# Three rounds of graph message passing on one core: a new order of the first blocks, larger first transfers and products of a constant at the beginning

## The chip, the cores and the metric

The kernel runs on one core of a Trainium2 chip. Its time is the device time of one execution in microseconds, as the median of several runs. An execution with the hardware profiler gives the trace; it has a span of its own, from the first to the last recorded event. Engines are called TensorE (PE in the rows, PEld for its weight loads), VectorE (DVE), ScalarE (ACT), GpSimd (POOL) and SyncE (SP, which here only issues DMAs).

## What is computed

x is 4096 x 128, adj is 4096 x 4096, both f32. A layer on a graph, a residual and a layer norm come first, then three rounds of two MLPs of three layers (without the last "vu" MLP, whose result is not used), a residual and a layer norm:

```python
x = _layernorm(x + relu((adj @ x) @ kernel + bias))
u = x
for _ in range(3):
    v = _mlp(adj @ u, uv_W1, uv_b1, uv_W2, uv_b2, uv_W3, uv_b3)
    u = _mlp(adj @ v, vu_W1, vu_b1, vu_W2, vu_b2, vu_W3, vu_b3)
return _layernorm(x + v)
```

Each multiplication with adj needs all of its 64 MB. There are six of them one after the other.

## The kernel before

**Blocks and uses.** adj is cut into 8 x 8 blocks of 512 x 512 (1 MB, 128 partitions of 2048 values). A *sweep* s is one multiplication with adj; row r of it makes chunk r of the result, and block (r, c) multiplies chunk c of the features. adj doesn't fit on the core, so a block that is loaded is used for sweep s ("finish") and, where the features of sweep s + 1 are there already, for that sweep too ("begin"). `block_products` lists these *uses*; for sweep 0 they stand in the table FIRST, written out by hand. There are 384 uses in all. Use n takes the ticks 4n to 4n + 3, a tick for each of the block's four tiles; all engines run over the same ticks in their own program.

**A use.** [...] A half of a block (two tiles, 128 x 1024) is copied by ScalarE from `adj_raw` to `adj_hi` (L593), and VectorE writes the difference to `adj_lo` (L722). TensorE multiplies adj_hi with feat_hi (L858) and feat_lo (L865) for two tiles, and then adj_lo with feat_hi (L872) for both: six products of 512 columns for a half, twelve for a use. The first block that needs a chunk of x brings it along (`brings_x`): x goes to `resid`, and is split by ScalarE (L587) and VectorE (L718).

**Buffers and queue.** `adj_raw` holds RAW = 8 halves, `adj_hi` and `adj_lo` hold RING = 4 blocks. SyncE issues all loads in the order of `plan.loads`. It waits until VectorE is through with the half that stood in the slot before; for the first WHOLE = 8 blocks one transfer brings both halves, and waits for both.

**Where the copies stand.** `Plan.due` gives the tick at which ScalarE and VectorE take up a half: its first use less a lead of FIRST_LEAD = 4 ticks for uses under 24 (FIRST_ROWS rows of 8), of LEAD = 12 ticks after that, and not before its place in the ring is free. Within a tick the steps of units come ahead of the halves in both programs. Whatever comes first in a program holds up what is behind it.

**Units.** When a row is closed, its chunk goes as a *unit* through the layers. For sweep 0 (kind GCN) the steps, counted in ticks from the tick after the close, are: ScalarE copies the bank (0), TensorE multiplies with the kernel (3, L769: four products of 128 columns), VectorE adds the bias (3, L689), adds the residual and takes mean and variance (5, L652, L606, L610), ScalarE takes the root (7, L518), VectorE scales (9, L617, L621), ScalarE writes feat_hi (11, L501) and VectorE feat_lo (12, L635). In the order before, units 0, 1, 2 and 3 close at uses 14, 16, 26 and 36 (counted from 0). Uses 19, 20, 24, 29, 30 and 37 are the ones that take a block already there.

Of the kernel before, what the change touches and what calls it, by code (L numbers as in the profile page):

```python
# [9 lines left out]
P = 128  # L10
# [16 lines left out]
DEEP = HIDDEN + (LAST,)  # L27
FINISH, BEGIN = "finish", "begin"

FIRST = (("finish", 1, (0,)), ("finish", 0, (6, 5, 1, 0)), ("finish", 2, (7,)), ("finish", 0, (7, 4, 3)),  # L30
         ("finish", 1, (7, 5, 2, 6, 1)), ("finish", 0, (2,)), ("finish", 1, (4, 3)), ("finish", 2, (0, 6)),
         ("begin", 2, (0,)), ("begin", 1, (0,)), ("finish", 2, (1, 4, 3)), ("begin", 2, (1,)),
         ("finish", 2, (5, 2)), ("finish", 3, (0,)), ("both", 3, (1,)), ("begin", 3, (0,)),
         ("finish", 3, (7, 4, 3, 6, 5)), ("both", 3, (2,)), ("finish", 4, (0, 1)), ("begin", 4, (0,)),
         ("finish", 4, (2, 7, 6, 5, 4, 3)), ("begin", 4, (1, 3, 2)), ("both", 5, (0, 1, 2, 3)),
         ("finish", 5, (7, 6, 5)), ("both", 5, (4,)), ("both", 6, (0, 1, 2, 3, 4)), ("finish", 6, (7, 6)),
         ("both", 6, (5,)))
WHOLE = 8
HOLD = 3
LEAD, FIRST_LEAD, FIRST_ROWS = 12, 4, 3  # L40
LOAD_GCN, LOAD_PARAMS = 24, 90
W_SPLIT = 320

# [27 lines left out]
def block_products(rows):  # L71
# [20 lines left out]
    for s in range(PASSES - 1):  # L92
        if s == 0:
            for what, r, columns in FIRST:
                yield from dict(finish=finish, begin=begin, both=both)[what](s, r, columns)
# [25 lines left out]
class Plan:  # L121


    def __init__(self, rows):
# [61 lines left out]
        for h, (b, i, _) in enumerate(self.loads):  # L186
            if b >= WHOLE or i == 0:
                signals[h % RAW] += 1
# [4 lines left out]
        for h, (b, i, pieces) in enumerate(self.loads):  # L193
            for j in range(pieces):
                self.load_at[b, i + j] = h
            first = self.first_use(b)
            free = 0 if self.before[b] is None else self.ends[self.before[b]] * TILES + i + pieces
            lead = FIRST_LEAD if first < FIRST_ROWS * rows else LEAD
            due = max(free, first * TILES + i - lead)
            turns = [t for (step, t), u in self.steps.items() if step == "dve_in" and self.steps_of(u) == TURN]  # L200
            self.due.append(next((t for t in turns if t - HOLD < due < t), due))
# [69 lines left out]
def gnn_kernel(nc, x, adj, weights, bias_rows, out):  # L271
# [12 lines left out]
    with ctx:  # L284
        def sb(name, shape, dt=F32):
            return ctx.enter_context(nc.sbuf_tensor(name, shape, dt))

        def ps(name, shape):
            return ctx.enter_context(nc.psum_tensor(name, shape, F32))
# [29 lines left out]
        one_row = sb("one_row", [P, P])  # L319
# [4 lines left out]
        pre_ps = ps("pre_ps", [P, CHUNK])  # L324
# [7 lines left out]
        one_row_ready = sem("one_row_ready")  # L332
# [42 lines left out]
        def tiles_of(u):  # L375
            return range(*plan.units[u][2])
# [76 lines left out]
        def _(sp):  # L453
            for h, (b, i, pieces) in enumerate(plan.loads):
# [9 lines left out]
                if h >= RAW:  # L464
                    sp.wait_ge(adj_lo_ready, h - RAW + (2 if b < WHOLE and i == 0 else 1))
                row, col = plan.blocks[b]
                if b < WHOLE:
                    if i == 0:
# [258 lines left out]
        def _(pe):  # L727
# [27 lines left out]
            def piece(i):  # L755
                return slice(i * CHUNK, (i + 1) * CHUNK)

            n_feats, h_hi, h_lo = 0, -1, -1
            for t in range(plan.ticks + TAIL):
                u = at(t, "pe_out", (GCN,) + DEEP)  # L760
                if u is not None:
# [6 lines left out]
                    for k, j in enumerate(tiles_of(u)):  # L768
                        last = pe.matmul(layer_bank(2, u)[:, k * P:(k + 1) * P], hid2[:, j * P:(j + 1) * P],  # L769
                                         w_raw[:, OUT_W[kind_of(u)], :], start=not biased,  # L770
                                         stop=not biased or j == tiles_of(u)[-1])
# [61 lines left out]
                if n == len(plan.order) - 1:  # L833
# [14 lines left out]
                    for k in (k - 1, k):  # L848
                        last = pe.matmul(to, feat_hi[feats][:, tile(src, k)],
                                         adj_lo[:, plan.slot[b], k * CHUNK + cut.start:k * CHUNK + cut.stop],  # L850
                                         start=False, stop=i % 2 == 1 and k == TILES - 1)
                    if i % 2 == 1:
                        last.then_inc(half_used, 1)
                    continue
                start = plan.opens[n] and i == 0
                stop = plan.closes[g] == (n if n < len(plan.order) - 2 else n + 1) and i == TILES - 1

                pe.matmul(group_bank(g), feat_hi[feats][:, tile(src, i)], adj_hi[:, plan.slot[b], piece(i)],  # L858
                          start=start, stop=False)
                if i == 0 and b in plan.brings_x and s == 0 and into == FINISH:  # L860
                    pe.wait_ge(x_lo_ready, plan.xs.index(c) + 1)
                if made > n_feats:
# [3 lines left out]
                          start=False, stop=False)  # L866
# [34 lines left out]
```

## Time and profile before

| | |
|---|---|
| time, median of 3 runs | 1171.03 us (1170.98 to 1171.18) |
| span of the profiled execution | 1169.0 us |
| TensorE busy | 1154.0 us (99%) |
| VectorE busy | 738.2 us (63%) |
| ScalarE busy | 660.8 us (57%) |
| DMA | 261.60 MB, mean 224 GB/s |

Busy times are shares of the whole span; the stretch that the change touches is the first 120 us. In the timeline a row can merge several instructions of one kind that follow each other (x2, x8), and the second number is then the time from the start of the first to the end of the last. TensorE's products are pipelined: the distance from one start to the next is what one costs, and not its duration.

### The profile page before, as it was taken

The numbers are of one execution on the slowest core, as the hardware profiler recorded it, in microseconds if no ns is written. First come the engines' busy times: TensorE is split into PE (matmuls) and PEld (weight loads), VectorE is DVE, ScalarE is ACT, GpSimd is POOL, SyncE is SP. The second block draws the span as 40 slices with busy tenths as digits, with TensorE's granted clock in tenths as the row PEclk, the third lists the DMA queues.
The fourth block names the chain that finished last, engine by engine and source line by source line (L and its number), as shares of the span: only waits on it lengthen the run. The fifth ranks groups of instructions, "written<-read, shape, count | busy, mean of one in ns | idle before, by whom it ended". The sixth has DMA issues, their size and how long they took to land.

```text
span 1169.0 us, 13697 instructions
## 1 busy us (share of the span) xinstructions
PE 1154.0 (99%) x5236; PEld 953.1 (82%) x5236; DVE 738.2 (63%) x890; ACT 660.8 (57%) x809; POOL 0.2 (0%) x4
## 2 busy tenths in 40 slices
PE   7999999999999999999999999999999999999997
PEld 6888888888888888888888888888888888887776
DVE  7997676458564555555545756554566555658886
ACT  7765554346554555555444754554566454557885
POOL 0000000000000000000000000000000000000000
PEclk9999999999999999999999999999999999999999
DMA  9988775568466646555656736655665566569891
GB/s 383 405 299 327 244 270 192 206 215 288 124 207 209 215 161 214 198 185 180 216 180 216 250 118 216 214 173 181 210 222 188 190 205 209 193 217 362 296 323 50
DMA packets 72210, 261.60 MB, mean 224 GB/s; under 512 B 8017, under 2 KB 8657, under 8 KB 71121
## 3 DMA queue, kind: packets, MB, share of 16 engines
q1 hardware_dynamic: 72000, 260.61, 64.2%
q8 instruction: 41, 0.67, 0.2%
q14 instruction: 25, 0.20, 0.0%
q10 hardware_dynamic: 144, 0.13, 0.0%
HBM read 258.61 MB, written 2.10 MB: 223 GB/s over the span
## 4 chain that ended last, share of the span: by engine, by line
PE 92%; DMA 3%; DVE 2%; ACT 2%; issue 1%; SPq 0%; DVEq 0%; ACTq 0%
PE agg_ps L872 28%; PE agg_ps L865 28%; PE agg_ps L858 28%; PE pre_ps L769 4%; DMA adj_raw<-in_adj 3%; PE hid_ps L730 1%; PE hid_ps L732 1%; PE hid_ps L731 1%; DVE adj_lo L722 1%; ACT adj_hi L593 1%; PE hid_ps L791 1%; PE hid_ps L805 0%; DVE stats L606 0%; ACT hid L487 0%; ACT resid L508 0%
## 5 line engine op out<-in xcount | busy, mean ns | idle before, releaser
L722 DVE TENSOR_TENSOR adj_lo<-adj_raw,adj_hi 128x1024 fp32r<-128x1024 f32 x488 | 576.7, 1220 | 230.2 <-ACT adj_hi L593 224.0
L858 PE MATMUL agg_ps<-adj_hi,feat_hi 128*128 128x512 f32 x1532 | 607.7, 397 | 7.4 <-ACT adj_hi L593 7.4
L865 PE MATMUL agg_ps<-adj_hi,feat_lo 128*128 128x512 f32 x1532 | 598.0, 390 | 0.0
L593 ACT ACTIVATE adj_hi<-adj_raw 128x1024 fp32r<-128x1024 f32 x488 | 492.8, 1052 | 94.8 <-PE agg_ps L872 80.3
L872 PE MATMUL agg_ps<-adj_lo,feat_hi 128*128 128x512 f32 x1532 | 473.8, 390 | 0.2 <-DVE adj_lo L722 0.2
L858 PEld LDWEIGHTS agg_ps<-adj_hi,feat_hi 128*128 128x128 f32 x1532 | 288.5, 188 | 68.8 <-issue 10.2
L865 PEld LDWEIGHTS agg_ps<-adj_hi,feat_lo 128*128 128x128 f32 x1532 | 288.5, 188 | 62.2 <-issue 3.4
L872 PEld LDWEIGHTS agg_ps<-adj_lo,feat_hi 128*128 128x128 f32 x1532 | 287.8, 188 | 61.9 <-DVE adj_lo L722 1.5
L487 ACT ACTIVATE hid<-hid_ps,params 128x512 f32<-128x512 f32 (+1 forms) x80 | 54.5, 681 | 59.1 <-PE hid_ps L732 50.6
L558 ACT ACTIVATE in_hi<-part 128x512 fp32r<-128x512 f32 x24 | 15.2, 634 | 110.3 <-DVE part L711 110.3
L487 ACT ACTIVATE post<-pre 128x512 f32<-128x512 f32 x39 | 24.6, 630 | 79.8 <-DVE pre L689 79.8
L689 DVE TENSOR_TENSOR pre<-pre_ps,b_row 128x512 f32<-128x512 f32 x47 | 32.4, 690 | 50.4 <-PE pre_ps L769 50.4
L711 DVE TENSOR_TENSOR part<-part,agg_ps 128x512 f32<-128x512 f32 (+1 forms) x31 | 20.6, 665 | 66.8 <-PE agg_ps L872 65.1
L769 PEld LDWEIGHTS pre_ps<-params,hid 128*128 128x128 f32 x380 | 49.9, 191 | 4.0
L769 PE MATMUL pre_ps<-params,hid 128*128 128x128 f32 x380 | 50.3, 275 | 0.0
L580 ACT ACTIVATE part<-agg_ps 128x512 f32<-128x512 f32 x30 | 17.9, 596 | 25.6 <-PE agg_ps L872 22.3
L558 ACT ACTIVATE in_hi<-agg_ps 128x512 fp32r<-128x512 f32 x8 | 4.8, 597 | 47.0 <-PE agg_ps L872 47.0
L702 DVE TENSOR_TENSOR in_lo<-agg_ps,in_hi 128x512 fp32r<-128x512 f32 x8 | 5.5, 690 | 40.7 <-ACT in_hi L558 40.7
L697 DVE TENSOR_TENSOR hid_lo<-hid,hid_hi 128x512 fp32r<-128x512 f32 x32 | 21.9, 685 | 12.2 <-ACT hid L487 12.2
L487 ACT ACTIVATE hid_hi<-hid_ps,params 128x512 fp32r<-128x512 f32 x32 | 21.9, 685 | 10.6 <-PE hid_ps L732 10.6
L679 DVE TENSOR_TENSOR feat_lo<-post,feat_hi 128x512 fp32r<-128x512 f32 x32 | 22.0, 686 | 8.6 <-ACT feat_hi L487 8.6
L702 DVE TENSOR_TENSOR in_lo<-part,in_hi 128x512 fp32r<-128x512 f32 x24 | 16.5, 689 | 11.9 <-ACT in_hi L558 11.9
(70 smaller groups left out, 262.2 us busy)
## 6 DMA issues: line engine op xcount, KB each, us to landing
adj_raw<-in_adj SPq DMA_DIRECT2D x472, 512.0 KB, 5.7
adj_raw<-in_adj SPq DMA_DIRECT2D x8, 1024.0 KB, 8.1
resid<-in_x SPq DMA_DIRECT2D x8, 256.0 KB, 8.0
out<-resid SPq DMA_DIRECT2D x7, 256.0 KB, 6.8
params<-in_weights SPq DMA_DIRECT2D x1, 386.0 KB, 4.7
b_row<-in_bias_rows SPq DMA_DIRECT2D x1, 128.0 KB, 5.5
out<-resid ACTq DMA_DIRECT2D x1, 128.0 KB, 2.1
out<-resid SPq DMA_DIRECT2D x1, 128.0 KB, 2.2
```

Source lines behind the costliest of these rows:

```text
L487: return act.activation(to, of, ACT.Prelu, alpha=SLOPE, **bias)
L593: act.activation(adj_hi[:, plan.slot[b], i * CHUNK:(i + pieces) * CHUNK], adj_raw[:, h % RAW, 0:pieces * CHUNK], ACT.Copy).then_inc(adj_hi ...
L679: dve.tensor_tensor(feat_block(feat_lo, u), post[:, :], feat_block(feat_hi, u).bitcast(F32), ALU.subtract).then_inc(feat_lo_ready, 1)
L689: dve.tensor_tensor(by_tile(pre[:, own(u)]), by_tile(layer_bank(2, u)), b_row[:, b * P:(b + 1) * P].rearrange("p (j f) -> p j f", f=P) .to ...
L697: dve.tensor_tensor(hid_lo[:, :], hid1[:, :], hid_hi[:, :].bitcast(F32), ALU.subtract)\
L702: dve.tensor_tensor(in_lo[:, :], agg(u), in_hi[:, :].bitcast(F32), ALU.subtract)\
L711: dve.tensor_tensor(agg(u), agg(u), agg_bank(u), ALU.add).then_inc(sum_kept, 1)
L722: dve.tensor_tensor(adj_lo[:, plan.slot[b], slot], adj_raw[:, h % RAW, 0:pieces * CHUNK], adj_hi[:, plan.slot[b], slot].bitcast(F32), ALU. ...
L769: last = pe.matmul(layer_bank(2, u)[:, k * P:(k + 1) * P], hid2[:, j * P:(j + 1) * P], w_raw[:, OUT_W[kind_of(u)], :], start=not biased, s ...
L858: pe.matmul(group_bank(g), feat_hi[feats][:, tile(src, i)], adj_hi[:, plan.slot[b], piece(i)], start=start, stop=False)
L865: pe.matmul(group_bank(g), feat_lo[feats][:, tile(src, i)], adj_hi[:, plan.slot[b], piece(i)], start=False, stop=False)
L872: last = pe.matmul(group_bank(g), feat_hi[feats][:, tile(src, k)], adj_lo[:, plan.slot[b], piece(k)], start=False, stop=stop and k == i)
```

## The change

The first rows of FIRST are reordered, so that rows 0 to 2 advance together by columns, from column 7 down to column 0. The 8 chunks of x are brought by 8 of the first 18 blocks (uses 0, 3, 5, 8, 10, 13, 15 and 17), before by 8 of the first 12. Each of the uses 0 to 22 takes a new block; 23, 25, 30, 31, 33 and 37 take one that is there. Units 0 to 2 close at uses 17, 22 and 28, unit 3 at use 36 as before. From use 38 on the order of uses is the same. WHOLE goes from 8 to 28, so that one transfer of 1 MB brings each block up to the one of use 29. The lead is 4 ticks for uses up to 33, grows by a tick every two uses, and is 12 from use 48 on. At its beginning TensorE makes 14 products of the constant `one_row` with itself (128 x 128, f32), whose result nothing reads.

```diff
-FIRST = (("finish", 1, (0,)), ("finish", 0, (6, 5, 1, 0)), ("finish", 2, (7,)), ("finish", 0, (7, 4, 3)),
-         ("finish", 1, (7, 5, 2, 6, 1)), ("finish", 0, (2,)), ("finish", 1, (4, 3)), ("finish", 2, (0, 6)),
-         ("begin", 2, (0,)), ("begin", 1, (0,)), ("finish", 2, (1, 4, 3)), ("begin", 2, (1,)),
-         ("finish", 2, (5, 2)), ("finish", 3, (0,)), ("both", 3, (1,)), ("begin", 3, (0,)),
-         ("finish", 3, (7, 4, 3, 6, 5)), ("both", 3, (2,)), ("finish", 4, (0, 1)), ("begin", 4, (0,)),
+FIRST = (("finish", 0, (7,)), ("finish", 1, (7,)), ("finish", 2, (7,)), ("finish", 0, (6,)), ("finish", 1, (6,)),
+         ("finish", 0, (5,)), ("finish", 1, (5,)), ("finish", 2, (6,)), ("finish", 0, (4,)), ("finish", 1, (4,)),
+         ("finish", 0, (3,)), ("finish", 1, (3,)), ("finish", 2, (5,)), ("finish", 0, (2,)), ("finish", 1, (2,)),
+         ("finish", 0, (1,)), ("finish", 1, (1,)), ("finish", 0, (0,)), ("finish", 2, (4, 3)), ("finish", 3, (7, 6)),
+         ("both", 1, (0,)), ("both", 2, (0,)), ("finish", 2, (2,)), ("finish", 3, (5,)), ("finish", 2, (1,)),
+         ("both", 3, (0,)), ("begin", 2, (1,)), ("both", 3, (1,)), ("finish", 3, (4, 3)), ("both", 3, (2,)),
+         ("finish", 4, (0, 1)), ("begin", 4, (0,)),
...
-WHOLE = 8
+WHOLE = 28
+WARM = 14
 HOLD = 3
-LEAD, FIRST_LEAD, FIRST_ROWS = 12, 4, 3
+LEAD, FIRST_LEAD, FIRST_USES = 12, 4, 32
...
-            lead = FIRST_LEAD if first < FIRST_ROWS * rows else LEAD
+            lead = min(LEAD, FIRST_LEAD + max(0, first - FIRST_USES) // 2)
...
+            pe.wait_ge(one_row_ready, 1)
+            for _ in range(WARM):
+                pe.matmul(pre_ps[:, 0:P], one_row[:, :], one_row[:, :], start=True, stop=True)
```

## Rows read from the trace of the kernel before

**Rows 1.** The page's head: busy time by engine, and the granted clock in 40 slices.

```profile
PE 1154.0 (99%) x5236; PEld 953.1 (82%) x5236; DVE 738.2 (63%) x890; ACT 660.8 (57%) x809; POOL 0.2 (0%) x4
PEclk9999999999999999999999999999999999999999
```

**Rows 2.** Table of waits: who waited for whom, us in total, times, longest.

```profile
PE agg_ps L858 <- ACT adj_hi L593: 7.4, 1, 7.4
```

**Rows 3.** Timeline, TensorE's first products: start us, us, what.

```profile
7.36 0.76 PE L858 MATMUL agg_ps<-adj_hi,feat_hi 128*128 128x512 f32 x1 [7.36 <-ACT adj_hi L593]
...
13.32 0.39 PE L858 MATMUL agg_ps<-adj_hi,feat_hi 128*128 128x512 f32 x1
...
26.50 0.39 PE L858 MATMUL agg_ps<-adj_hi,feat_hi 128*128 128x512 f32 x1
```

**Rows 4.** Timeline, TensorE at uses 11, 12, 17 and 18.

```profile
40.09 0.39 PE L858 MATMUL agg_ps<-adj_hi,feat_hi 128*128 128x512 f32 x1
...
44.49 0.40 PE L858 MATMUL agg_ps<-adj_hi,feat_hi 128*128 128x512 f32 x1
...
59.02 0.39 PE L858 MATMUL agg_ps<-adj_hi,feat_hi 128*128 128x512 f32 x1
...
60.84 0.39 PE L858 MATMUL agg_ps<-adj_hi,feat_hi 128*128 128x512 f32 x1
...
64.63 0.39 PE L858 MATMUL agg_ps<-adj_hi,feat_hi 128*128 128x512 f32 x1
```

**Rows 5.** Timeline, products of unit 0 with the kernel (L769) and what follows.

```profile
53.13 1.06 PE L769 MATMUL pre_ps<-params,hid 128*128 128x128 f32 x8
53.94 0.48 PE L858 MATMUL agg_ps<-adj_hi,feat_hi 128*128 128x512 f32 x1
```

**Rows 6.** Timeline of VectorE.

```profile
1.10 0.17 DVE L602 MEMSET one_row<- 1x128 f32 x1
7.25 2.36 DVE L722 TENSOR_TENSOR adj_lo<-adj_raw,adj_hi 128x1024 fp32r<-128x1024 f32 x2 [2.33 <-ACT adj_hi L593]
...
55.36 0.68 DVE L689 TENSOR_TENSOR pre<-pre_ps,b_row 128x512 f32<-128x512 f32 x1
55.97 1.22 DVE L722 TENSOR_TENSOR adj_lo<-adj_raw,adj_hi 128x1024 fp32r<-128x1024 f32 x1
57.10 0.68 DVE L652 SCALAR_TENSOR_TENSOR post<-pre,resid 128x512 f32<-128x512 f32 x1
...
59.02 1.19 DVE L722 TENSOR_TENSOR adj_lo<-adj_raw,adj_hi 128x1024 fp32r<-128x1024 f32 x1
...
61.56 0.17 DVE L617 RECIPROCAL rstd<-std 128x4 f32<-128x4 f32 x1
...
62.79 1.22 DVE L722 TENSOR_TENSOR adj_lo<-adj_raw,adj_hi 128x1024 fp32r<-128x1024 f32 x1
...
98.50 13.71 DVE L722 TENSOR_TENSOR adj_lo<-adj_raw,adj_hi 128x1024 fp32r<-128x1024 f32 x12
```

**Rows 7.** Timeline of ScalarE, copies that wait for 1 MB transfers.

```profile
6.16 2.00 ACT L593 ACTIVATE adj_hi<-adj_raw 128x1024 fp32r<-128x1024 f32 x2 [1.96 <-DMA adj_raw<-in_adj]
...
18.13 2.01 ACT L593 ACTIVATE adj_hi<-adj_raw 128x1024 fp32r<-128x1024 f32 x2 [0.49 <-DMA adj_raw<-in_adj]
21.27 2.01 ACT L593 ACTIVATE adj_hi<-adj_raw 128x1024 fp32r<-128x1024 f32 x2 [0.61 <-DMA adj_raw<-in_adj]
23.76 2.01 ACT L593 ACTIVATE adj_hi<-adj_raw 128x1024 fp32r<-128x1024 f32 x2 [0.47 <-DMA adj_raw<-in_adj]
```

**Rows 8.** Timeline of ScalarE, a wait for half a block, and a copy of a bank.

```profile
34.02 1.06 ACT L593 ACTIVATE adj_hi<-adj_raw 128x1024 fp32r<-128x1024 f32 x1 [1.52 <-DMA adj_raw<-in_adj]
...
51.51 0.60 ACT L569 ACTIVATE hid<-agg_ps 128x512 f32<-128x512 f32 x1
```

**Rows 9.** Busy time by stretches; the last two columns are DMA share and GB/s.

```profile
8.00:20.00 12.00, 12.00 (x44) 9.64 (x43) 11.26 (x12) 9.61 (x12) 0.00 (x0) 1.00 1.02 419
40.00:58.00 18.00, 18.00 (x84) 14.61 (x83) 16.81 (x16) 14.09 (x14) 0.00 (x0) 1.00 1.03 409
```

## The prediction, made before the changed kernel ran

> **What bounds the kernel now.** I read five views in this order. The page's head gives TensorE 99% of the span [rows 1]. The table of waits gives its only long idle time, 7.4 us ahead of the first product [rows 2]. So the time is a sum of products at their pitch, plus what the beginning and the tail add; the tail is not touched. The timeline of TensorE is then read for pitches and not for waits: a use of a block is 12 products, and 60 products between 26.50 and 40.09 us give 13.59/60 = 0.2265 us each, 2.718 us a use [rows 3]. Pitches also show what the table of waits leaves out, since a late weight load appears as a longer pitch:
>
> - The first 14 products take 13.32 - 7.36 = 5.96 us, at a pitch of 0.425 us, where 14 x 0.2265 is 3.17 [rows 3]. That is 2.79 us lost. [...]
> - Three places later are too long [rows 4]: use 11 and half of use 12 (40.09 to 44.49: 4.40 for 18 products, 4.08, so 0.32), half of use 17 (59.02 to 60.84: 1.82 for six, 1.36, so 0.46), and use 18 (60.84 to 64.63: 3.79 for twelve products, 2.72, and 0.91 for a unit's product, which part 3 takes from its row, so 0.16). Together 0.94 us. I found none from there to use 38.
>
> So nothing over 2.79 + 0.94 = 3.7 us is to be had. What matters is what the supply (the DMA queue, then ScalarE's copy, then VectorE's difference) can do when TensorE is up to 2.8 us earlier.
>
> **Part 1, the constant products.** 14 products of 128 columns in f32; the trace shows such products as two records each, eight in 53.94 - 53.13 = 0.81 us at full clock [rows 5]. 28 records are 2.8 us at full and 5.7 us at half clock. one_row is ready at 1.27 us [rows 6], so they end near 7.0 us, ahead of 7.36: they cost nothing, and the cover is the first block's way in. [...] I take the first real product as fast. Gain: -2.79 us, and -0.94 because every stall of before is counted anew below.
>
> **Part 2, the supply of the first 18 uses.** The first 18 uses of the new order are 18 different blocks, 8 of them with a chunk of x. A block of 1 MB follows the one before by 23.76 - 21.27 = 2.49 us, and by 3.14 with an x (21.27 - 18.13), so an x is 0.65 [rows 7]. The first block is in at 6.16 us. Block 17 is in at 6.16 + 17 x 2.49 + 7 x 0.65 + 0.3 = 53.3 us; 0.3 is the two parameter loads ahead of block 12 (0.13 MB at 409 GB/s [rows 9]). From a landing to the difference of its first half goes 1.09 us for the copy and its signal (6.16 to 7.25) and 1.22 for the difference [rows 6, 7]; TensorE resumes some 0.18 us behind that (a difference ends at 59.02 + 1.19 = 60.21, and the pair that waits for it counts from 60.84 - 0.45 = 60.39) [rows 4, 6]. It wants that half 0.91 us into the use, so use 17 can't start before 53.3 + 1.09 + 1.22 + 0.18 - 0.91 = 54.9 us. Without any stall it would start at 7.36 + 17 x 2.718 = 53.57. So TensorE loses **1.35 us**, in steps of 0.2 to 0.3 us at uses that bring x. VectorE doesn't set this: 2 x 1.135 us a block and 0.6 an x are 45.7 us for 18 blocks [rows 6], against 48.9.
>
> Bounds: at the 409 GB/s of the later stretch a block takes 2.56 us [rows 9]; that makes it 1.35 + 17 x 0.07 = 2.6. If the early 419 GB/s [rows 9] rose by 2%, blocks would be in by 0.9 sooner, and it would be about 0.5. I take 2.49, since blocks 5 to 7 came at it with all engines at full pace. WHOLE = 28 keeps this form until use 29. It also avoids the change of form of before, where the halves after block 7 came late (a copy waits 1.52 us up to 34.02) [rows 8]. [...]
>
> **Part 3, the units' work between blocks.** Each unit sends VectorE work of 0.61 (55.36 to 55.97), 1.92 (57.10 to 59.02), 1.23 (61.56 to 62.79) and again 0.61 us [rows 6], and ScalarE's copy of its bank, through queues that also carry the blocks. With a lead of 4 ticks (one use) a block's copies stand just behind them. In the old order unit 0 had the new blocks of uses 17 and 18 under it, and then came uses of blocks already there (19, 20); now uses 18 to 22 are all new blocks, and 24, 26, 27 and 28 too. Worked out from the start S of use 18, in program order:
>
> - ScalarE waits for unit 0's bank until S + 0.2 (an estimate for the signal, as the 0.18 above), copies it (the row is 0.60 long [rows 8], the next starts 0.5 behind it), then block 19: VectorE begins it 1.09 later, at S + 1.8, its second half at 2.93, pre at 4.07, block 20's first half at 4.68, the statistics at 5.82 for 1.92 us. Call the end E = S + 7.74. Block 20's second half is in use at E + 1.22 + 0.18 = S + 9.14; TensorE is there at S + 2 x 2.718 + 0.91 (unit 0's product, 53.94 + 0.10 - 53.13) + 2.27 = S + 8.61. **0.53 us**. The same place of the old order is use 17, which lost 0.46 [rows 4].
> - std (0.2), the copy of block 21's first half, its difference, reciprocal and scaling (1.23), and the difference of its second half: in the old order this took from 59.02 to 64.63 - 0.45 = 64.18, or 5.16 us with the late weight load [rows 4, 6]. TensorE is there 1.40 + 2.72 = 4.12 us behind E. **1.04 us**. In the old order unit 1's product (0.91) lay between them, so 5.03 stood against 5.16, and 0.16 was lost [rows 4]. This is the best tested term.
> - Behind the scaling ScalarE makes feat_hi (0.54, a copy of the same size as the bank's), then the copy (1.09), and VectorE needs 1.40: 3.15 us behind the scaling for block 22's first half, with the first bullet's 1.40 + 1.36 = 2.76 against it. **0.39 us**. In the old order the next new block was two uses off.
> - Unit 1 closes at use 22. From the start S of use 23: copy of the bank, block of use 24 from 1.8 on, pre 4.07, statistics 4.8, E = S + 6.7, plus 5.16 is 11.86; TensorE is at the second half of use 26 at 0.91 + 3 x 2.718 + 2.27 = 11.33. **0.53**, and again **0.39** at use 27.
> - Unit 2 closes at use 28; the next new block is at use 32. Nothing. From use 38 on both orders are the same; the smaller lead there (7 to 12 ticks) costs nothing that I can find: the supply has slack, as the loads follow at 1.135 us while a use of 2.72 needs two.
>
> Sum of part 3: 0.53 + 1.04 + 0.39 + 0.53 + 0.39 = **2.9 us**. It does not hang on the DMA rate: each term stands against TensorE's own position. Bounds: 1.3 if the third term and unit 1 find slack that I don't see, 3.4 if each chain is 0.1 longer.
>
> **Sum.** -2.79 - 0.94 + 1.35 + 2.9 = +0.5 us. The profiled execution spans 1169.0 us and the median is 1171.03, 2.0 more around the span. Span 1169.5, time **1171.5 us**.
>
> **Rivals.**
>
> 1. The constant products don't raise the clock in time. Then use 17 starts at 53.57 + 2.79 = 56.4 instead of 54.9 (the supply's stalls vanish under it), part 3 stays: +2.0, 1173.0. For it: nothing in the trace shows such products from rest. Against: 5.7 us of them fit the slow stretch seen. A rise that costs up to 1.35 us more costs nothing, since the supply sets use 17. Chance 0.09.
> 2. Slower than before, the supply: transfers of 1 MB under full flow fall back to 2.56 us a block and the lag that before shows at 34.02 us (1.52 us of waiting, 0.2 of it usual, so 1.3) [rows 8] comes here as well. Use 17 then starts at 54.9 + 1.2 + 1.3 = 57.4: +3.0, 1174.0. It decides the sign by my bound once block 17 lands later than 55.2 us. For it: the queue frees 1 MB only when both halves are used. Against: blocks 4 to 7 already ran so, at 2.49. Chance 0.11.
> 3. Faster: the early landings come 2% sooner in the new order, so that the supply costs 0.3 instead of 1.35, and of part 3 only the two places of unit 0 that the old order shows count, with the first at 0.46 and the second at half its price, 0.52: -3.72 + 0.3 + 1.0 = -2.4, 1168.6. It decides the sign by my bound only if both hold. For it: my chains take signals at 0.1 to 0.2 us each, which add up. Against: the losses of uses 17 and 18 of before are met by the same sums within 0.1 us. Chance 0.16.
>
> **How the numbers follow.** Forecast 0.64, rivals 0.09, 0.11 and 0.16. The forecast alone spans 1170.1 to 1172.8. A measurement of this kernel tells 0.2%, 2.3 us, from no change: faster is under 1168.7, slower over 1173.4. Faster gets 0.12 (most of rival 3), slower 0.14 (rival 2 and a part of rival 1), same 0.74. The range reaches from 1168.6 to 1173.6.
>
> **What would show it.** Products at a pitch of 0.2265 from the first one on (part 1). Copies that start every 2.49 and 3.14 us to about 53.3 us, and TensorE's late weight loads at uses 5, 10, 13, 15 and 17 (part 2). Pitches too long near 67, 71, 72, 86 and 88 us, the largest at 71 (part 3). Use 38, where the orders meet again, starts 0.5 us later than before. I am wrong if block 17 lands after 55 us, if the statistics of unit 0 don't delay a block, or if the first products still stand at 0.425.

## The result

| | median | runs | span of the profiled execution |
|---|---|---|---|
| before | 1171.11 us (1170.88 to 1171.26) | 8 | 1169.0 us |
| after | 1174.1 us (1173.65 to 1174.52) | 8 | 1172.7 us |

The ratio is 1.0026, with a 95% interval of 1.0017 to 1.0035: the changed kernel is 3.0 us slower, where 0.5 was forecast. The median lies above the stated range of 1168.6 to 1173.6. The profiled execution of after was its slowest, 1174.52 us, 0.4 above the median, so its trace holds 3.5 to 3.7 us more than that of before.

**The profile after.** All readings are from the stretch up to use 38. Lines have moved by 3 above TensorE's program, by 7 in it: L593 is now L596, L722 is L725, L858, L865, L872 and L769 are L865, L872, L879 and L776. The page's head; it answers to [rows 1]:

```profile
PE 1161.0 (99%) x5264; PEld 955.6 (81%) x5264; DVE 738.2 (63%) x890; ACT 659.6 (56%) x809; POOL 0.2 (0%) x4
```

TensorE is busy 7 us longer, and 5.9 of that are the constant products. The timeline of TensorE at the beginning, which answers to [rows 3], and the start of use 17:

```profile
1.32 5.89 PE L763 MATMUL pre_ps<-one_row 128*128 128x128 f32 x28 [1.32 <-DVE one_row L605]
7.25 0.47 PE L865 MATMUL agg_ps<-adj_hi,feat_hi 128*128 128x512 f32 x1
...
8.98 0.39 PE L865 MATMUL agg_ps<-adj_hi,feat_hi 128*128 128x512 f32 x1
...
57.54 0.39 PE L865 MATMUL agg_ps<-adj_hi,feat_hi 128*128 128x512 f32 x1
...
119.89 1.06 PE L776 MATMUL pre_ps<-params,hid 128*128 128x128 f32 x8
```

The constant products are 28 records in 5.89 us and end by 7.2. No real product runs at the slow pitch of 0.425 us ([rows 3]; the granted clock doesn't tell the two apart: in before it is 1.00 from 7.36 to 13.32 us, over the 14 products at that pitch): the first six take 1.73 us (7.25 to 8.98), where six at 0.2265 are 1.36, and the 0.37 between are mostly waits for the first block's difference. From there the pitch is 0.2265. Use 17 starts at 57.54 us and not at 54.9. Unit 3's product, the last mark ahead of use 38, is at 119.89 us; in the trace of before the same row is at 116.33, so 3.56 us are lost by then:

```profile
116.33 1.06 PE L769 MATMUL pre_ps<-params,hid 128*128 128x128 f32 x8
```

The timeline of ScalarE: copies that wait for a transfer, which answer to [rows 7] and [rows 8]. The number in brackets is how long ScalarE waited.

```profile
22.32 2.01 ACT L596 ACTIVATE adj_hi<-adj_raw 128x1024 fp32r<-128x1024 f32 x2 [0.49 <-DMA adj_raw<-in_adj]
...
29.26 2.01 ACT L596 ACTIVATE adj_hi<-adj_raw 128x1024 fp32r<-128x1024 f32 x2 [1.85 <-DMA adj_raw<-in_adj]
31.79 2.01 ACT L596 ACTIVATE adj_hi<-adj_raw 128x1024 fp32r<-128x1024 f32 x2 [0.51 <-DMA adj_raw<-in_adj]
...
37.44 2.01 ACT L596 ACTIVATE adj_hi<-adj_raw 128x1024 fp32r<-128x1024 f32 x2 [0.49 <-DMA adj_raw<-in_adj]
41.70 2.01 ACT L596 ACTIVATE adj_hi<-adj_raw 128x1024 fp32r<-128x1024 f32 x2 [2.25 <-DMA adj_raw<-in_adj]
...
56.11 2.01 ACT L596 ACTIVATE adj_hi<-adj_raw 128x1024 fp32r<-128x1024 f32 x2 [0.59 <-DMA adj_raw<-in_adj]
```

A usual wait is 0.5 us (0.6 where an x came along). Two are not: block 8 at 29.26 us (1.85, so 1.2 to 1.3 too late) and block 12 at 41.70, 4.26 us after block 11 where 2.49 + 0.3 had been counted: 1.47 too late. Everything else keeps the pace, and block 17 is in at 56.1 instead of 53.3. That is the miss.

TensorE around 69 to 75 us, where unit 0's steps stand between the blocks:

```profile
69.10 0.39 PE L872 MATMUL agg_ps<-adj_hi,feat_lo 128*128 128x512 f32 x1
69.74 0.74 PE L879 MATMUL agg_ps<-adj_lo,feat_hi 128*128 128x512 f32 x2 [0.26 <-DVE adj_lo L725]
70.33 0.40 PE L865 MATMUL agg_ps<-adj_hi,feat_hi 128*128 128x512 f32 x1
...
72.42 0.39 PE L872 MATMUL agg_ps<-adj_hi,feat_lo 128*128 128x512 f32 x1
73.55 0.74 PE L879 MATMUL agg_ps<-adj_lo,feat_hi 128*128 128x512 f32 x2 [0.73 <-DVE adj_lo L725]
74.12 0.40 PE L865 MATMUL agg_ps<-adj_hi,feat_hi 128*128 128x512 f32 x1
```

From 69.10 to 70.33 three products take 1.23 us instead of 0.68: 0.55 lost, where 0.53 was forecast. From 72.42 to 74.12 they take 1.70: 1.02, forecast 1.04.

### The profile page after: what moved, and what is told of

The parts are those of the page before. It is cut to its first block, busy times and chain, and to the rows that moved or that the text cites. A ratio compares the mean times of both kernels' runs of the same rounds, so it can differ in the third digit from the quotient of the medians.

```text
span 1172.7 us, 13748 instructions
## 1 busy us (share of the span) xinstructions
PE 1161.0 (99%) x5264; PEld 955.6 (81%) x5264; DVE 738.2 (63%) x890; ACT 659.6 (56%) x809; POOL 0.2 (0%) x4
## 4 chain that ended last, share of the span: by engine, by line
PE 90%; DVE 4%; DMA 4%; ACT 2%; issue 1%; SPq 0%; DVEq 0%; ACTq 0%
PE agg_ps L879 27%; PE agg_ps L872 27%; PE agg_ps L865 27%; DMA adj_raw<-in_adj 4%; PE pre_ps L776 3%; DVE adj_lo L725 2%; ACT adj_hi L596 1%; PE hid_ps L733 1%; PE hid_ps L735 1%; PE hid_ps L734 1%; PE hid_ps L798 1%; DVE resid L624 0%; DVE stats L609 0%; PE hid_ps L812 0%; ACT hid L490 0%
## 5 line engine op out<-in xcount | busy, mean ns | idle before, releaser
L725 DVE TENSOR_TENSOR adj_lo<-adj_raw,adj_hi 128x1024 fp32r<-128x1024 f32 x488 | 576.5, 1222 | 240.7 <-ACT adj_hi L596 234.5
L865 PE MATMUL agg_ps<-adj_hi,feat_hi 128*128 128x512 f32 x1532 | 606.9, 396 | 1.4 <-ACT adj_hi L596 1.4
L872 PE MATMUL agg_ps<-adj_hi,feat_lo 128*128 128x512 f32 x1532 | 597.2, 390 | 0.0
L596 ACT ACTIVATE adj_hi<-adj_raw 128x1024 fp32r<-128x1024 f32 x488 | 491.3, 1052 | 95.8 <-PE agg_ps L879 80.2
L879 PE MATMUL agg_ps<-adj_lo,feat_hi 128*128 128x512 f32 x1532 | 474.3, 391 | 1.4 <-DVE adj_lo L725 1.2
L879 PEld LDWEIGHTS agg_ps<-adj_lo,feat_hi 128*128 128x128 f32 x1532 | 286.4, 188 | 66.5 <-DVE adj_lo L725 7.2
L865 PEld LDWEIGHTS agg_ps<-adj_hi,feat_hi 128*128 128x128 f32 x1532 | 287.8, 188 | 64.2 <-issue 4.5
L872 PEld LDWEIGHTS agg_ps<-adj_hi,feat_lo 128*128 128x128 f32 x1532 | 287.8, 188 | 61.9 <-issue 3.4
L776 PEld LDWEIGHTS pre_ps<-params,hid 128*128 128x128 f32 x380 | 49.9, 191 | 4.0
L776 PE MATMUL pre_ps<-params,hid 128*128 128x128 f32 x380 | 50.3, 275 | 0.0
L572 ACT ACTIVATE hid<-agg_ps 128x512 f32<-128x512 f32 x8 | 4.8, 596 | 36.8 <-PE agg_ps L879 36.8
```

What stands on the lines that cost most here:

```text
L596: act.activation(adj_hi[:, plan.slot[b], i * CHUNK:(i + pieces) * CHUNK], adj_raw[:, h % RAW, 0:pieces * CHUNK], ACT.Copy).then_inc(adj_hi ...
L725: dve.tensor_tensor(adj_lo[:, plan.slot[b], slot], adj_raw[:, h % RAW, 0:pieces * CHUNK], adj_hi[:, plan.slot[b], slot].bitcast(F32), ALU. ...
L872: pe.matmul(group_bank(g), feat_lo[feats][:, tile(src, i)], adj_hi[:, plan.slot[b], piece(i)], start=False, stop=False)
L879: last = pe.matmul(group_bank(g), feat_hi[feats][:, tile(src, k)], adj_lo[:, plan.slot[b], piece(k)], start=False, stop=stop and k == i)
```

## What the loss is made of

By the same reading of pitches as in the prediction, for the profiled executions up to unit 3's product:

| term | forecast | measured in after |
|---|---|---|
| slow first products | -2.79 | -2.79, and a first product 0.11 sooner |
| late weight loads of before | -0.94 | -0.94 |
| supply up to the start of use 17: 57.54 - 7.25 - 17 x 2.718 | +1.35 | +4.08 |
| three late products in uses 17 and 18 (58.8, 61.5, 61.8 us) | 0 | +0.4 |
| unit 0: uses 20, 21, 22 | 0.53, 1.04, 0.39 | 0.55, 1.02, 0.34 |
| unit 1: uses 26, 27 | 0.53, 0.39 | 0.54, 0.35 |
| sum | +0.5 | +3.44 of 3.56 |

The first row holds for these two executions. Without the constant products the number of slow products differs from one to the next: 14 in before, 12 in b_nog, 10 in a_nowarm, and 9 in b_order, where they cost 1.8 us instead of 2.79. One trace can't show that.

## Experiments

Each changes one thing against before (names with b) or after (names with a). Times are medians; before was 1171.0 to 1171.2 us beside each of them. The intervals of the ratios are about 0.0009 to either side, or 1.1 us.

**Is the slow beginning on the path?** The constant products alone:

```diff
+            pe.wait_ge(one_row_ready, 1)
+            for _ in range(14):
+                pe.matmul(pre_ps[:, 0:P], one_row[:, :], one_row[:, :], start=True, stop=True)
```

> The kernel before with nothing but the 14 constant products ahead of TensorE's program. Theory A, the supply of blocks sets TensorE's pace up to use 18: VectorE runs without a gap from 51.6 us on in the kernel before, so the differences that TensorE waits for at 60.2 and 64.0 us stay where they are, and a start that is 2.8 us earlier turns into waits ahead of them: 1171.0, within 0.3 us of before, with the first products at a pitch of 0.2265. Theory B, the slow first products are on the path: 2.8 us less, 1168.3.

1171.78 us, ratio 1.0007 (0.9998 to 1.0016). The 2.8 us that the fast first products bring (second one at 7.67, pitch 0.23) buy nothing. In the timelines of b_warm, TensorE then waits for block 7, and the late place of use 17 is there as in [rows 4] (0.45 us). Block 7:

```profile
28.47 2.01 ACT L593 ACTIVATE adj_hi<-adj_raw 128x1024 fp32r<-128x1024 f32 x2 [2.16 <-DMA adj_raw<-in_adj]
...
27.88 0.62 PE L876 MATMUL agg_ps<-adj_lo,feat_hi 128*128 128x512 f32 x2
29.67 0.47 PE L862 MATMUL agg_ps<-adj_hi,feat_hi 128*128 128x512 f32 x1 [1.17 <-ACT adj_hi L593]
```

The 2.8 us go in waits for the supply. Use 9 starts at 35.65 us (34.66 before), and 1.7 us of the waits up to it stand at block 7 alone, which is the late one here; from there to use 17 hardly a product is late. Unit 3's product is at 117.00 us for 116.33, so this trace, too, is 0.7 us longer, though the interval of the medians just includes no change. The other side of it is the changed kernel without the products:

```diff
-            pe.wait_ge(one_row_ready, 1)
-            for _ in range(WARM):
-                pe.matmul(pre_ps[:, 0:P], one_row[:, :], one_row[:, :], start=True, stop=True)
```

> The changed kernel without its 14 constant products. Theory A, the supply sets the beginning: block 17 lands at about 56 us as in after, TensorE comes 2.8 us later to the early blocks and waits less; 1174.1, within 0.4 us. Theory B, the clock is on the path: 2.8 us more, less the waits that vanish (2.6 us in after up to use 17), if they are waits for the same blocks.

1173.93 us, 0.2 less than after: no difference. The time is that of theory A, but the way there is not quite: two differences cancel. ScalarE in a_nowarm, blocks 12, 17 and 20:

```profile
40.97 2.01 ACT L596 ACTIVATE adj_hi<-adj_raw 128x1024 fp32r<-128x1024 f32 x2 [1.17 <-DMA adj_raw<-in_adj]
...
55.43 2.01 ACT L596 ACTIVATE adj_hi<-adj_raw 128x1024 fp32r<-128x1024 f32 x2 [0.60 <-DMA adj_raw<-in_adj]
...
64.00 2.01 ACT L596 ACTIVATE adj_hi<-adj_raw 128x1024 fp32r<-128x1024 f32 x2 [1.55 <-DMA adj_raw<-in_adj]
```

Block 12 is only 0.7 us late, block 17 is in 0.7 sooner than in after, and use 17 starts at 56.85 us instead of 57.54. Then block 20 is late, and the place of use 20 costs 1.1 us instead of 0.55. By unit 3's product 0.33 are left (119.56 us for 119.89). The slow first products cost nothing in sum, on either order, because the supply takes it up. My rival 1 had asked 2.0 - 0.5 = 1.5 us for it.

**What makes one block late?** My prediction put the lag of before at 34 us [rows 8] down to the change from 1 MB to half a block, and held that WHOLE = 28 avoids it. So WHOLE alone, in both directions:

```diff
-WHOLE = 8
+WHOLE = 28
```

> The kernel before with WHOLE = 28, order and lead as before. My prediction held that the form of the transfers makes the lag at 34.02 us; by it the lag of 1.3 us goes, blocks 8 to 17 land 1.3 to 2 us sooner, and the 0.94 us of late weight loads vanish: 1170.2. Theory A, the lag comes from TensorE's own instruction fetch of 16 KB, which holds one of the 16 DMA engines for 1.1 us (31 to 32 us in before, 24 to 25 in after): a landing 1.3 us late stays, and the emptier queue at the parameter loads (35 to 37 us in after) comes in too: 1171.1 to 1172.5.

1172.71 us, ratio 1.0014 (1.0004 to 1.0023): slower, not faster, and 0.2 above what theory A allowed. The late block is still there, with transfers of 1 MB throughout, at 39.44 us; a second one follows at 43.40, behind the two small loads. ScalarE in b_whole:

```profile
39.44 2.01 ACT L593 ACTIVATE adj_hi<-adj_raw 128x1024 fp32r<-128x1024 f32 x2 [1.85 <-DMA adj_raw<-in_adj]
43.40 2.01 ACT L593 ACTIVATE adj_hi<-adj_raw 128x1024 fp32r<-128x1024 f32 x2 [1.95 <-DMA adj_raw<-in_adj]
```

The other direction is after with WHOLE = 8:

> The changed kernel with WHOLE = 8 again. Theory C, the large transfers cost the second late landing (41.70 us instead of about 40.2), since the queue holds less when the parameter loads come: with halves it is 0.4 us instead of 1.8, and blocks after the seventh take 2.56 instead of 2.50 us: 1173.3. By my prediction's view, in which the change from 1 MB to halves makes a lag of its own: 1.3 + 0.6 us more than after, 1176.

1174.31 us: no difference from after (neither 1173.3 nor 1176). The form of the transfer is not the reason. Theory C missed as well: with halves the small loads cost 1.1 us there (a half lands 2.34 us after the one before it, at 40.55) and not 0.4.

What the traces have in common shows in the DMA view of a short stretch. Before, 31.5 to 32.0 us, and after, 24.5 to 25.0 us (queue: packets, MB, share of 16 engines):

```profile
q1 hardware_dynamic: 52, 0.19, 97.1%
q8 instruction: 1, 0.02, 13.8%
...
q1 hardware_dynamic: 85, 0.24, 123.5%
q8 instruction: 1, 0.02, 13.7%
```

The one packet of the queue "instruction" takes 13.8% of 16 engines for 0.5 us, 1.1 us of one engine's time. Over the whole kernel before the page has this queue with 41 packets of 16 KB:

```profile
q8 instruction: 41, 0.67, 0.2%
```

TensorE has 5236 + 5236 = 10,472 recorded matmul and weight-load instructions [rows 1], 255 for a packet, so I took the packets for fetches of TensorE's instructions. The blocks keep the DMA share at 1.02 and 1.03 [rows 9], and my estimate from these numbers was that 1.1 us of one engine's time, taken out of a queue that is never empty, makes a landing behind it about that much late. No view shows single engines, so how a packet does this isn't shown. But if the packets are TensorE's and cause the lag, more instructions for TensorE must move the late block. They were added as waits on a semaphore that is long set:

```diff
+            for _ in range(100):
+                pe.wait_ge(one_row_ready, 1)
```

> The kernel before with 100 waits on a semaphore that is long set at the beginning of TensorE's program, while TensorE idles anyway. They are instructions and nothing else. Theory A, a late landing follows each fetch of 16 KB (256 of TensorE's instructions): the fetch of 31 us comes at about 20 us, the one of 58 us at about 47, a block lands 1.3 to 1.5 us late behind each, and both lie ahead of use 17: 0.7 to 1.5 us slower, 1172.2. Rival, the lag of 34 us comes with the change of form of the transfers or at a fixed time: it stays at 34 us, time as before.

1171.63 us. The count of instructions grows by 50 (13697 to 13747), and not by 100 as I had expected; 50 are 50/24 x 2.718 = 5.7 us of TensorE's stream. The fetch comes at 26.0 us (31.5 before), and the late landing moves to 28.36:

```profile
28.36 2.01 ACT L593 ACTIVATE adj_hi<-adj_raw 128x1024 fp32r<-128x1024 f32 x2 [2.12 <-DMA adj_raw<-in_adj]
```

The late landing moved with the fetch, and nothing but TensorE's instructions had changed; the size of the shift was wrong for the number of waits. The second fetch (56.6 us) comes after block 17 is in. The time is 0.6 us longer, not clear of noise, and unit 3's product is later by as much (116.95 us). The same with 300:

> The kernel before with 300 waits at the beginning of TensorE's program. 100 of them made 50 more instructions and moved the fetch from 31 to 26 us and the late landing from 34.0 to 28.4, as 50 instructions at 24 to a use of 2.72 us make 5.7 us. So 150 instructions: fetches near 14 and 42 us, late landings of 1.3 to 1.5 us near 16 and 44 us; both lie ahead of use 17, whose differences come later by up to 1.3: 1172.3. Rival: one late landing at about 28 us stays, whatever the count.

1180.3 us, and this run tells something else: TensorE's first product is at 17.61 us, since 300 waits take it 16 us. Of 10.25 us of delay 9.2 show in the time. The supply is then far ahead (only four copies up to 45 us wait for a transfer), and nothing can be read about late landings. The fetch comes 5.9 us after the first product; before it was 24.1, so 150 more instructions moved it by 18 us where 17.0 were worked out. The run is void for the question of landings.

The constant products as 4 instructions of up to 512 columns:

```diff
-            for _ in range(WARM):
-                pe.matmul(pre_ps[:, 0:P], one_row[:, :], one_row[:, :], start=True, stop=True)
+            for k in (4, 4, 4, 2):
+                pe.matmul(by_tile(pre_ps[:, 0:k * P]), one_row[:, :],
+                          one_row[:, :].rearrange("p (j f) -> p j f", f=P).to_broadcast([P, k, P]),
+                          start=True, stop=True)
```

> The changed kernel with its constant products in 4 instructions of up to 512 columns instead of 14 of 128: the same columns, some 20 to 40 fewer instructions for TensorE. Theory A: the fetch comes 2.3 to 4.5 us later than at 24.8 us, the late block is 9 or 10 and not 8, the clock is up at the first real product as in after, and the time stays at 1174.1 within 0.4.

1174.41 us, within what was expected. The constant products end by 7.2 us (5.83 us), and the first real one is at 7.37 us, with a pitch of 0.23 from the second (7.68 us) on. The fetch is at 28.0 us, and block 8 is on time; block 9 is late:

```profile
28.08 2.01 ACT L596 ACTIVATE adj_hi<-adj_raw 128x1024 fp32r<-128x1024 f32 x2 [0.61 <-DMA adj_raw<-in_adj]
31.81 2.01 ACT L596 ACTIVATE adj_hi<-adj_raw 128x1024 fp32r<-128x1024 f32 x2 [1.72 <-DMA adj_raw<-in_adj]
```

The first fetch (start of the half microsecond that holds it) and the first late landing:

| kernel | fetch, us | late copy starts, us | waited, us |
|---|---|---|---|
| after | 24.5 | 29.26 | 1.85 |
| a_whole8 | 24.5 | 28.60 | 0.74 and more |
| b_waits | 26.0 | 28.36 | 2.12 |
| b_warm | 26.0 | 28.47 | 2.16 |
| a_warm4 | 28.0 | 31.81 | 1.72 |
| before | 31.5 | 34.02 | 1.52 |
| b_order | 31.5 | 34.09 | 1.85 |
| a_nowarm | 33.0 | 35.40 | 2.10 |
| b_whole | 34.5 | 39.44 | 1.85 |

(In a_whole8 ScalarE makes an x's copy inside the wait.) The other kernels that come from after have the fetch at 24.5 us and the late copy at 29.3 to 29.6, and b_nog stands within 0.1 us of before. In each the landing that comes 2.4 to 5 us behind the fetch is the late one, by 1.2 to 1.6 us, and no other up to use 17 is, but for the small loads. Counted in TensorE's recorded instructions up to the start of that half microsecond, with the 50 and 150 of the waits, the first fetch comes behind 191 to 207 in all kernels, b_waits300 among them, but b_whole (219); in time it lies anywhere from 23.8 to 34.8 us. Why a landing follows after 2.4 us in one and 4.9 in another I can't say; how far the transfers overlap in the queue was not measured. Nor was a kernel run without a fetch: it could be moved, not left out.

**The second late block.** Its neighbour in the queue is the pair of loads for the first layer, 128 KB in rows of 512 bytes. They were moved to block 16:

```diff
-LOAD_GCN, LOAD_PARAMS = 24, 90
+LOAD_GCN, LOAD_PARAMS = 32, 90
```

> The changed kernel with the two loads for the first layer (128 KB in rows of 512 bytes) ahead of block 16 instead of block 12. Theory D, these two loads themselves cost the DMA engines 1.5 us and not 0.3: block 12 lands on time (some 1.4 us sooner than in after), block 16 late by as much; from use 17 on nothing differs, 1174.1 within 0.4. Rival E, block 12 is late because block 8 is: its issue waits for the difference of block 8, and the queue runs low: block 12 stays late with nothing ahead of it, and block 16 loses 0.3.

1174.11 us, as theory D has it. Block 12 lands on time, block 16 doesn't:

```profile
39.95 2.01 ACT L596 ACTIVATE adj_hi<-adj_raw 128x1024 fp32r<-128x1024 f32 x2 [0.49 <-DMA adj_raw<-in_adj]
...
48.81 2.01 ACT L596 ACTIVATE adj_hi<-adj_raw 128x1024 fp32r<-128x1024 f32 x2 [0.67 <-DMA adj_raw<-in_adj]
52.85 2.01 ACT L596 ACTIVATE adj_hi<-adj_raw 128x1024 fp32r<-128x1024 f32 x2 [2.02 <-DMA adj_raw<-in_adj]
```

4.04 us where 2.49 is usual: 1.55 for the two loads. Rival E falls. Issued by ScalarE, on a queue of their own:

```diff
-                if h == LOAD_GCN:
-                    sp.dma_start(params[:, 0:P], weights[:, 0:P]).then_inc(gcn_loaded, 16)
-                    sp.dma_start(b_row[:, 0:P], bias_rows[0:P].partition_broadcast(P)).then_inc(gcn_loaded, 16)
...
+                if t == 24:
+                    act.dma_start(params[:, 0:P], weights[:, 0:P]).then_inc(gcn_loaded, 16)
+                    act.dma_start(b_row[:, 0:P], bias_rows[0:P].partition_broadcast(P)).then_inc(gcn_loaded, 16)
```

> The changed kernel with the two loads in rows of 512 bytes issued by ScalarE near 24 us, on its own queue, instead of by SyncE ahead of block 12. Theory D, the cost lies in the DMA engines, which move these rows slowly: a block lands late by 1 to 1.5 us near 28 us instead of block 12 near 41, and the time stays, 1174.1. Rival F, the cost is the place in SyncE's queue, where block 12 can't follow before they are written out: no block is late for them, use 17 comes 1.3 us sooner, 1172.8.

1173.82 us: again the time stays. Busy time by stretches in a_gcnact (DMA share and GB/s are the last two columns):

```profile
29.00:30.00 1.00, 0.76 (x4) 0.30 (x2) 0.00 (x0) 0.45 (x1) 0.00 (x0) 1.00 1.01 399
30.00:31.00 1.00, 0.25 (x1) 0.28 (x2) 0.37 (x1) 1.00 (x2) 0.00 (x0) 1.00 0.46 76
31.00:32.00 1.00, 1.00 (x5) 0.48 (x4) 1.00 (x2) 0.56 (x1) 0.00 (x0) 1.00 0.90 344
```

For a microsecond the engines move 76 GB/s, and are busy less than half of it. Blocks 9, 10 and 11 are hardly moved in the meantime, though SyncE had issued them by 28.4 us and they stand in another queue (q1, at 40.5% of 16 engines in this microsecond; the two loads in q10, at 5.5%). Block 8 is 0.3 us and block 9 1.0 us later for it. In after it is the stretch from 35 to 37 us:

```profile
35.00:36.00 1.00, 1.00 (x6) 0.84 (x5) 0.84 (x2) 1.00 (x2) 0.00 (x0) 1.00 0.89 283
36.00:37.00 1.00, 1.00 (x7) 0.79 (x5) 0.97 (x1) 0.95 (x1) 0.00 (x0) 1.00 0.59 230
```

Against the usual 418 GB/s (after from 42 to 43 us) this is 0.32 MB short in two microseconds, 0.8 us. At the 409 GB/s of [rows 9] the two loads would take 0.3 us, the estimate that I had counted with. The landings say 1.55 to 1.8 here, and the measurement decides. Neither load was run alone, so it is open whether the short rows do it, or the one row of bias that is read for all 128 partitions.

How much of the loss goes with them, and does before pay as well? Both kernels without the two loads, with constants in their place:

```diff
-                if h == LOAD_GCN:
-                    sp.dma_start(params[:, 0:P], weights[:, 0:P]).then_inc(gcn_loaded, 16)
-                    sp.dma_start(b_row[:, 0:P], bias_rows[0:P].partition_broadcast(P)).then_inc(gcn_loaded, 16)
...
+            dve.memset(b_row[:, 0:P], 0.0)
+            dve.memset(params[:, 0:P], 0.01).then_inc(gcn_loaded, 1)
...
-                        pe.wait_ge(gcn_loaded, 32)
+                        pe.wait_ge(gcn_loaded, 1)
```

> The changed kernel without the two loads for the first layer: its weights and bias are filled with constants at the beginning instead (the real values are left out). Theory D: block 12 lands 1.4 to 1.8 us sooner, the waits of after at 41.6 to 44.1 us go, use 17 starts near 56.0 instead of 57.5, and 1.3 us less than after remain: 1172.8. If it is the queue that had run low for another reason: block 12 stays late, 1174.1.

1172.26 us (1172.8 expected), 1.84 less than after. Block 12 lands at 40.08, block 17 at 54.56, and use 17 starts at 55.95 us, 1.59 sooner than in after.

> The kernel before with the same loads left out. Its TensorE comes 2.8 us later, so the cover should hide most of them: the landing at 41.54 us comes 0.4 to 0.5 us sooner, the late weight loads at 43.9 and 59.7 shrink, 0.3 us less, 1170.8. If these loads cost before as much as after, it is 1169.7, and they are no reason for the difference between the two.

1170.46 us, 0.7 less than before, ratio 0.9994 (0.9984 to 1.0003). The landing of 41.54 us is now 41.19. Before, and then b_nog:

```profile
41.54 1.06 ACT L593 ACTIVATE adj_hi<-adj_raw 128x1024 fp32r<-128x1024 f32 x1 [0.63 <-DMA adj_raw<-in_adj]
...
41.19 1.06 ACT L590 ACTIVATE adj_hi<-adj_raw 128x1024 fp32r<-128x1024 f32 x1 [0.21 <-DMA adj_raw<-in_adj]
```

TensorE's late weight loads add up to 0.88 us for 0.94, and unit 3's product is at 116.23 us for 116.33. So before pays 0.1 us for the two loads by the traces and 0.7 by the medians, whose interval includes nothing at all; after pays 1.8. I had put this down to TensorE's late start, as a cover. The landings say otherwise: in before the two loads delay the blocks themselves by 0.35 us only. Their price on the queue is not a fixed one. By the landings of block 12 (of 16 in a_gcn32) it is:

| kernel | late by the two loads, us |
|---|---|
| before | 0.35 |
| a_nowarm | 0.7 |
| a_whole8 | 1.1 |
| b_whole | 1.5 |
| a_gcn32 | 1.55 |
| after | 1.8 |
| b_order | 2.5 |

What decides between 0.35 and 2.5 us wasn't found. The form alone doesn't: before, a_whole8 and b_order all have halves there. So the price of the two loads in after is measured, and why before pays so much less stays open.

**Do the units' steps hold up the blocks?** Units 0 and 1 with less work on VectorE:

```diff
-                for j in tiles_of(u):
+                for j in (0,) if u < 2 else tiles_of(u):
                     last = dve.bn_stats(stats[:, j, :], post_of(u)[:, j * P:(j + 1) * P])
...
-                    last = dve.bn_aggr(mean_var[:, j, :], stats[:, j, :])
+                    last = dve.bn_aggr(mean_var[:, j, :], stats[:, 0 if u < 2 else j, :])
...
-                for j in tiles_of(u):
+                for j in (0,) if u < 2 else tiles_of(u):
                     last = dve.tensor_scalar(of_chunk[:, j * P:(j + 1) * P], post_of(u)[:, j * P:(j + 1) * P],
```

> The changed kernel, where units 0 and 1 take the statistics of one tile for all four and scale one tile of four: a part of the layer norm of two chunks is left out. VectorE saves 0.66 + 0.83 us in each of the two units. Part 3: the late weight loads at 69, 72, 75, 88 and 90 us (0.55, 1.02, 0.34, 0.54, 0.35) depend on these steps; each chain gets shorter by 0.66 up to the end of the statistics and by 0.83 behind it, so the second goes down by 0.8, the first by 0.5, those of unit 1 go: 2.4 us less, 1171.7. Rival, the landings of blocks 19 to 22 set these places: no change, 1174.1.

1171.74 us, 2.4 less than after and the expected time within 0.1. What unit 0 costs TensorE comes down from 1.91 us to 0.50 (0.16 at 71.4, 0.34 at 72.9), and unit 1's places are gone. The landings up to use 17 are those of after. Part 3 of the prediction is shown by this.

The old rule for the lead:

```diff
-            lead = min(LEAD, FIRST_LEAD + max(0, first - FIRST_USES) // 2)
+            lead = FIRST_LEAD if first < 24 else LEAD
```

> The changed kernel with the old rule for the lead: 4 ticks for blocks first used before use 24, 12 from there. My prediction's part 3, unit 1's steps hold up the blocks of uses 26 and 27 because these stand just behind them: the late weight loads of after at 88.4 and 90.3 us (0.54 and 0.35) go, 0.9 us less than after, 1173.2. Rival, VectorE has too much to do there whatever its order: the same 0.9 us come out elsewhere, 1174.1.

1173.35 us, 0.75 less than after (0.9 expected, both within the noise of such a difference). The trace is plain: behind unit 0's last place at 75 us no late weight load is left up to 118 us. With 12 ticks the copies of uses 26 and 27 stand ahead of unit 1's steps.

**The order of uses by itself**, on the kernel before:

```diff
-FIRST = (("finish", 1, (0,)), ("finish", 0, (6, 5, 1, 0)), ("finish", 2, (7,)), ("finish", 0, (7, 4, 3)),
...
+FIRST = (("finish", 0, (7,)), ("finish", 1, (7,)), ("finish", 2, (7,)), ("finish", 0, (6,)), ("finish", 1, (6,)),
...
```

> The kernel before with the new order of uses alone: transfers of half a block after block 7, the old lead (12 ticks from use 24 on), no constant products. By the sums of part 3 with the supply as measured (a fetch lag of 1.3 us in it), unit 0's three places cost 0.53 + 1.04 + 0.39, where before loses 0.94 in all; TensorE starts slow and is not held by the supply otherwise: 1.0 to 1.2 us slower than before, 1172.2. Rival, the order is the whole loss: 1174.1.

1173.73 us, ratio 1.0022 (1.0013 to 1.0031). I had expected 1172.2. Unit 0's three places are there as counted (0.70, 1.00 and 0.35 us), but the supply costs more than I had put in: the fetch lag (34.09 us, 1.85 waited) and the small loads (41.51, 2.69 waited) make some 4 us together. That exceeds the 1.8 us by which TensorE's slow start holds it back here, and a product of TensorE is 0.86 us late at 42.6, with steps of 0.2 to 0.3 after that. The order by itself is thus 2.6 of the 3.0 us, and the other three parts, added to it, cost 0.4, less than an interval. The parts don't simply add up: WHOLE = 28 costs 1.7 us on the old order and nothing on the new one.

## Why the prediction was wrong

**Part 1** held in each number: 28 records of 5.9 us for 5.7, an end at 7.2 for 7.0, no slow real product. Its factor of two was an estimate; measured, the constant records take 0.210 us each (5.89/28) against 0.101 in unit 0's product [rows 5], and the products of 512 columns 0.425 us against 0.2265 [rows 3], a factor of 2.1 and of 1.9. But its gain is worth nothing. By part 2 the supply asked 1.35 of the 2.79 us back; it took all of it, in b_warm as in after.

**Part 3** held: 2.8 us for 2.9, each of the five terms within 0.05, and a_less and a_lead24 show their causes. These sums could be tested beforehand on two places of the kernel before, which is why they came out.

**Part 2** failed, in the step "block 17 is in at 6.16 + 17 x 2.49 + 7 x 0.65 + 0.3 = 53.3 us". Its pace was right: blocks land every 2.49 and 3.15 us. Two terms beside it were wrong.

- The lag at 34.02 us [rows 8] was read as the price of changing from 1 MB to halves, "avoided" by WHOLE = 28. b_whole and a_whole8 show that it isn't. It follows the fetch of TensorE's instructions, which every kernel here has once ahead of use 17: 1.3 us, in after as well. The step took a wait for the price of what stood beside it.
- The two small loads stood at 0.3 us, from their bytes. In after they make block 12 1.8 us late; a_gcn32 has 1.55 for them, and a_nog takes 1.84 us off the time. In before the term would have been right (0.35), and why it isn't in after is open.

Beyond the forecast they make 1.3 + 1.5 = 2.8 us, block 17 at 56.1. Rival 2 had half of the mechanism (a lag of before that comes in after too), at a chance of 0.11. That its time, 1174.0, is nearly the measured one is luck: its other 1.2 us were a pace of 2.56 us a block, which did not come. The trace of before had a better bound, since its first 18 blocks, 8 chunks of x and two loads are the same bytes. Its two halves of block 17:

```profile
54.33 1.06 ACT L593 ACTIVATE adj_hi<-adj_raw 128x1024 fp32r<-128x1024 f32 x1 [0.21 <-DMA adj_raw<-in_adj]
55.62 1.06 ACT L593 ACTIVATE adj_hi<-adj_raw 128x1024 fp32r<-128x1024 f32 x1 [0.23 <-DMA adj_raw<-in_adj]
```

I explained 1.0 us of the first and 2.3 us of the second away by the form of the transfers, with no row for it. With 54.33 in place of 53.3 the sum would have given +1.5 us. With 55.6, when the whole block was in, as a transfer of 1 MB needs it, it would have given +2.8 (both are estimates by the prediction's own sum), and the range would have reached past 1174.

**The ceiling** was the other thing to see. In the trace of before use 17 starts at 57.66 us with unit 0's product (0.91) ahead of it, so at 56.75 without, and by the same sum as in part 2 its supply allows 54.33 + 2.49 - 0.91 = 55.9. So, by this estimate, some 0.8 us were in reach up to there of the 3.7 that I called the most to be had, and b_warm got none of them. No run here beats the kernel before by more than b_nog does, which leaves work out.

## To carry to other kernels

Where a stage is bound by its supply, add up what arrived by a given time in the trace of before, instead of building it from the best pace of single transfers. What a slow start of the consumer loses can then be free, because it would wait for the supply anyway. Work that is queued between copies of a lead of one use costs what it lasts as soon as no use of a present block follows; write out the chain in program order and test the sum at a place where the old trace already has it. A wait that is several times its neighbours' needs a cause with a row of its own before it is counted out.

## What the runs showed of the hardware

- A fetch of TensorE's instructions is a packet of 16 KB on q8 "instruction" that takes 1.0 to 1.1 us of one DMA engine's time (12.9 to 14.0% of 16 engines in 0.5 us, in the kernels of the table); before has 41 in its 1169.0 us, one for 28.5 us and for 255 of the 10,472 recorded instructions. 50 more instructions for TensorE moved the first from 31.5 to 26.0 us (b_waits). With the blocks' queue at 78.1 (b_warm) to 127.9% (b_whole) of 16 engines in the same half microsecond, the landing 2.4 to 5 us behind it was 1.2 to 1.6 us late.
- Two loads of 64 KB in rows of 512 bytes, on the blocks' queue, made the blocks behind them late by 0.35 us (before) to 2.5 (b_order), and by 1.8 in after; on a queue of their own the rate of all engines fell to 76 GB/s for a microsecond (a_gcnact, 30 to 31 us).
- Behind 14 products of a nearly empty constant (5.9 us, after), or 4 with the same number of columns (5.8 us, a_warm4), no product of 512 columns has the slow pitch of 0.425 us, and the pitch goes to 0.2265. Without them the first 14 (before), 12 (b_nog), 10 (a_nowarm) and 9 (b_order) have it. The page's granted clock reads 1.00 in both cases, and only the pitch shows the difference.
- 300 waits on a semaphore that is set took TensorE 16 us (1.3 to 17.6, b_waits300), some 54 ns each, at a time when it would have been idle for the first 6.
